# A graph network kernel on one core: the first two layers rearranged around edge counting

## What is computed

```python
h = relu(layernorm(x));  agg = segment_sum(h[src], dst)
x = x + relu((h + agg) @ L0_W1 + b1) @ L0_W2 + b2            # layer 0
h = relu(layernorm(x));  h = relu(h @ L1_W1 + b1) @ L1_W2 + b2   # hidden 64
x = x + h + segment_sum(h[dst], src)                          # layer 1
h = relu(layernorm(x))                                        # layer 2
cond = silu([sin(ph), cos(ph)] @ f_w1 + f_b1) @ f_w2 + f_b2   # ph: node_vec1 * 32 frequencies
for i in range(4):        # sparse attention over the edges, 4 heads
    y = norm(h) * (1 + cond @ s1_w + s1_b) + (cond @ b1_w + b1_b);  h = h + attention(y)
    y = the same with s2, b2;  h = h + relu(y @ m_w1 + m_b1) @ m_w2 + m_b2
x = x + h
x = x + L3(relu(layernorm(x)))   # 2 attention layers, 8 heads, edges turned round, then an MLP
```

## Time and profile before

| | us |
|---|---|
| median of 3 runs | 1182.97 (1182.5 to 1183.24) |
| profiled execution: its own time | 1185.03 |
| profiled execution: span | 1183.2 |
| mean granted clock of TensorE | 0.972 |
| busy: PE / weight loads | 1083.8 (92%) / 995.4 |
| busy: DVE / POOL / ACT | 809.2 (68%) / 710.6 (60%) / 548.9 (46%) |
| PE's share of the chain of waits that ended last | 65% |

### The profile page before, as it was taken

How to read it: one execution, slowest core, us unless ns; L and a number is a source line. 1 busy time by engine, 2 the same in 40 slices (tenths; PEclk the granted TensorE clock), 3 DMA queues, 4 the chain that set the end, 5 groups by cost and what they waited for, 6 DMA issues and landing times.

```text
span 1183.2 us, 20938 instructions
## 1 busy us (share of the span) xinstructions
PE 1083.8 (92%) x6814; PEld 995.4 (84%) x6814; DVE 809.2 (68%) x1562; ACT 548.9 (46%) x970; POOL 710.6 (60%) x960
## 2 busy tenths in 40 slices
...
GB/s 121 2 1 1 10 25 37 91 104 55 49 34 46 81 57 81 1 82 46 55 81 1 81 85 6 79 122 53 94 1 37 72 2 45 1 72 37 36 1 44
DMA packets 39358, 56.99 MB, mean 48 GB/s; under 512 B 13829, under 2 KB 14079, under 8 KB 38877
## 3 DMA queue, kind: packets, MB, share of 16 engines
...
## 4 chain that ended last, share of the span: by engine, by line
PE 65%; DVE 4%; POOL 4%; issue 2%; ACT 1%; POOLq 0%; DVEq 0%; ACTq 0%
PE ps L312 39%; PE ps L1610 8%; PE ps L334 7%; PE ps L1904 3%; PE ps L1923 3%; PE ps L2086 2%; PE ps L1870 1%; PE ps L1584 1%; POOL w_lo L352 1%; POOL prob L431 1%; ACT prob L408 1%; DVE prob L401 1%; POOL res L1291 0%; DVE acc L1809 0%; DVE acc L1807 0%
## 5 line engine op out<-in xcount | busy, mean ns | idle before, releaser
L352 POOL TENSOR_TENSOR w_lo<-w_raw,w_hi 128x512 fp32r<-128x512 f32 x152 | 202.8, 1334 | 12.7
L312 PE MATMUL ps<-yt_hi,w_hi 128*128 128x314 f32 x640 | 201.3, 314 | 4.0 <-DVE yt_lo L1988 3.8
L312 PE MATMUL ps<-yt_hi,w_lo 128*128 128x314 f32 x640 | 197.3, 308 | 0.0
L312 PE MATMUL ps<-yt_lo,w_hi 128*128 128x314 f32 x640 | 197.0, 308 | 0.0
L431 POOL TENSOR_SCALAR prob<-prob,rinv 125x628 f32<-125x628 f32 x160 | 126.9, 795 | 105.9 <-DVE rinv L416 87.0
L375 ACT ACTIVATE pt_hi<-ps 125x625 fp32r<-125x625 f32 x160 | 109.3, 694 | 103.2 <-PE ps L334 102.0
L349 POOL TENSOR_SCALAR w_hi<-w_raw 128x512 fp32r<-128x512 f32 x152 | 96.2, 633 | 71.1 <-DMA w_raw<-L_gnn_wo 38.4
L668 PE MATMUL ps<-oh_s,oh_d 125*125 125x314 bf16 x800 | 117.3, 303 | 23.5 <-DVE oh_s L564 17.7
L668 PEld LDWEIGHTS ps<-oh_s,oh_d 125*125 125x125 bf16 x800 | 105.8, 138 | 34.6 <-DVE oh_s L564 22.9
L312 PEld LDWEIGHTS ps<-yt_hi,w_hi 128*128 128x128 f32 x640 | 121.4, 190 | 6.5 <-issue 3.5
L312 PEld LDWEIGHTS ps<-yt_hi,w_lo 128*128 128x128 f32 x640 | 121.4, 190 | 0.0
...
## 6 DMA issues: line engine op xcount, KB each, us to landing
...
```

The source lines that it names most:

```text
L312: ins = pe.matmul(out_ap, lhs(i, kk), rhs(j, kk), start=kk == 0 and n == 0, stop=kk == count - 1 and n == 2)
L352: pool.tensor_tensor(w[slot][1][:, kk, 0:cols], w_raw[slot][:, kk, 0:cols], w[slot][0][:, kk, 0:cols].bitcast(FP32), ALU.subtract).then_in ...
```

## The change

**Counting takes side jobs** (table `SIDE`). In chunks 1 and 2 PE also transposes the tiles of h (job h), in chunks 2 to 5 it multiplies them with W1 (job u), ahead of the last eight groups of the chunk ("5" stands behind the last chunk). ACT and DVE split the results. The copies of h itself (L646 and the subtraction) go. Each chunk's first matmul waits for the side splits of the earlier chunks.

```diff
+    SIDE = ((1, "h", 0), (1, "h", 1), (1, "h", 2), (2, "h", 3), (2, "h", 4), (2, "u", 0), (3, "u", 1), (3, "u", 2),
+            (4, "u", 3), (5, "u", 4))
...
+    def act_side(act, c):
+        for i, kind, t in side_jobs(c):
+            source, high, _ = side_parts(i, kind, t)
+            act.wait_ge(s_xf, i + 1)
+            act.activation(high, source, ACT.Identity).then_inc(s_eh0, 1)
+    def dve_side(dve, c):
+        for i, kind, t in side_jobs(c):
+            source, high, lower = side_parts(i, kind, t)
+            dve.wait_ge(s_eh0, i + 1)
+            dve.tensor_tensor(lower, source, high.bitcast(FP32), ALU.subtract).then_inc(s_el0, 1)
+    def pe_side(pe, c):
+        for i, kind, t in side_jobs(c):
+            ap = side_bank(i)
+            if kind == "h":
+                pe.wait_ge(s_hn0, t + 1)
+                for b in range(C):
+                    ins = pe.transpose(ap[:, 128 * b:128 * b + R], res[:, t, b * 128:(b + 1) * 128], ident[0:R, 0:R])
...
+            if side_jobs(c):
+                pe.wait_ge(s_below, c * TILES)
+                pe_side(pe, c)
...
+        pe_side(pe, CHUNKS)
...
-    agg = pair("agg", "qk", [128, C, W])
-    MASKS_AFTER_G, MASKS_AFTER_F = ((0, 1), (2, 3), (4,), (5, 6)), ((7,), (8,), (9,), ())
...
-    tail = ["o0", "o1", "o2", "c1", "o3", "y0", "o4", "y1", "r", "y2", "y3", "y4", "ga", "c2"]
...
+    names1 = "b0 - b1 b2 - b3 - - b4 - g0 g1 c1 g2 g3 o0 o1 o2 c2 o3 y0 o4 y1 r y2 y3 y4 - ga".split()
+    names1 += "p0 p1 p2 p3 p4".split()
```

**Layer 0**: g is now u times the counts, so f, `agg` and `rtmp` go. ACT takes the relu in PSUM (`g_relu`). The embedding's inputs are loaded early; the embedding, c1, `act_one` and c2 move forward. Only five masks are made; the other five are transposes of them by PE (m0 to m4, `act_turned`), in the first norm. SP and POOL:

```diff
+    def first_sp(sp):
+        sp.wait_ge(s_xf, len(SIDE))
+        load_w(sp, 0, "L2_gnn_wv", 0, s_wl2)
+        sp.wait_ge(s_float, 2 * TILES)
+        sp.dma_start(noise[:, 0:N], a["node_vec1"].rearrange("n a -> a n").to_broadcast([64, N])).then_inc(s_noise, 16)
+        sp.dma_start(b2row[:], row(a["L0_gnn_b2"])).then_inc(s_row1, 16)
+        sp.dma_start(b1row[:], a["L1_gnn_b1"].rearrange("(a n) -> a n", a=1).to_broadcast([R, HID])).then_inc(s_row1, 16)
...
+    def first_pool(pool):
+        steps = Steps(s_p1)
+        pool.wait_ge(s_float, 2 * TILES)
+        pool.memset(noise[:, N:W], 0.0).then_inc(s_k, 1)
+        pool.memset(act1[:], 1.0).then_inc(s_k, 1)
+        pool.wait_ge(s_row1, 32)
+        for t in range(TILES):
+            pool.tensor_tensor(x[:, t, :], x[:, t, :], b2row[:], ALU.add).then_inc(s_xb1, 1)
+        for t in range(TILES):
+            steps.done(pool.tensor_scalar(ai(0, t), cnt[:, t, :], 1.0, 1.0, ALU.mult, ALU.mult))
             steps.wait(pool)
...
+        def rstd_of(t, count):
+            pool.wait_ge(s_st1, count + t + 1)
+            pool_rstd(pool, steps, t, s_rs1)
+        pool.wait_ge(s_wl2[0], 16)
+        for t in range(TILES):
+            rstd_of(t, 0)
+            if t in (1, 2):
+                split_weights(pool, steps, 0, s_wsp[0], [t - 1])
+        jobs1.wait_filled(pool, f"o{TILES - 1}")
+        pool.memset(r_nat[0][:, :, HID:ONES].bitcast(FP32), 1.0).then_inc(s_w2, 1)
+        pool.memset(r_nat[1][:, :, HID:ONES].bitcast(FP32), 0.0).then_inc(s_w2, 1)
+        pool.wait_ge(s_wsl, WS_DMAS * 16)
+        pool.wait_ge(s_wsz, 64)
+        split_ws(pool, steps)
+        split_weights(pool, steps, 0, s_wsp[0], [2])
+        jobs1.wait_filled(pool, "ga")
+        for part in yt:
+            pool.memset(part[:, :, N:W].bitcast(FP32), 0.0).then_inc(s_w2, 1)
```

The bias additions on x now stand ahead of the splits of the counts. ACT's order, cut:

```diff
+        def g_relu(c):
+            s = jobs1.wait_filled(act, f"g{c}")
+            act.activation(wide(s), wide(s), ACT.Relu, bias=b0c[:, c:c + 1]).then_inc(s_gr, 1)
+            act.wait_ge(s_gr, c + 1)
+            act.activation(halves(ft[0][:, c, :]), wide(s), ACT.Copy).then_inc(s_h1, 1)
...
+        act.wait_ge(s_ang, 1)
+        act.activation(emb[:], phase[:], ACT.Sin).then_inc(s_sin, 1)
+        g_relu(0)
+        g_relu(1)
+        s = jobs1.wait_filled(act, "c1")
+        act.wait_ge(s_fw, 14 * 16)
+        act.activation(halves(pre[:]), wide(s, 0, COND), ACT.Identity, bias=f_b1[:, 0:1]).then_inc(jobs1.drained[s], 1)
+        jobs1.wait_drained(act, "c1")
+        act.activation(sig[:], pre[:], ACT.Exp, scale=-1.0).then_inc(s_ex1, 1)
+        g_relu(2)
+        log(0)
+        g_relu(3)
+        log(1)
+        norm(0, 0)
+        norm(1, 0)
+        s = jobs1.wait_filled(act, "c2")
+        act.activation(halves(cond[:]), wide(s), ACT.Copy).then_inc(s_c2, 1)
+        log(2)
+        norm(2, 0)
+        y_hi(0)
+        norm(3, 0)
+        y_hi(1)
+        norm(4, 0)
+        y_hi(2)
+        log(3)
+        y_hi(3)
+        r_hi(0, 0, 3)
+        y_hi(4)
+        log(4)
+        r_hi(1, 3, 5)
+        act.wait_ge(s_m, TILES)
+        s = jobs1.at["ga"][0]
+        jobs1.wait_filled(act, "ga")
+        for half in range(2):
+            act.activation(gt[0][0:ONES, H2 * half:H2 * half + H2], ps[s][0:ONES, 512 * half:512 * half + H2],
+                           ACT.Identity).then_inc(s_h1, 1)
+    def act_first_norm(act, t):
```

DVE's order, cut:

```diff
+        for t in range(TILES):
+            b_lo(t)
+        embed_noise()
+        clamp(0)
+        g_lo(0)
+        g_lo(1)
+        act_one()
+        g_lo(2)
+        make_mask(0)
+        clamp(1)
+        g_lo(3)
+        make_mask(1)
+        dve.wait_ge(s_xb1, TILES)
+        residual("o0", 0)
+        residual("o1", 1)
+        residual("o1", 1)
...
+        residual("o2", 2)
+        make_mask(2)
+        y_lo(0)
+        residual("o3", 3)
+        clamp(3)
+        y_lo(1)
+        residual("o4", 4)
+        dve.wait_ge(s_row1, 32)
+        y_lo(2)
+        make_mask(3)
+        clamp(4)
+        y_lo(3)
+        r_part(0, 0, 3)
+        y_lo(4)
+        r_lo(0, 0, 3)
+        make_mask(4)
+        r_part(1, 3, 5)
+        jobs1_r = jobs1.at["r"][0]
+        dve.wait_ge(s_rsum, 2)
+        dve.sem_inc(jobs1.drained[jobs1_r], 1)
+        r_lo(1, 3, 5)
```

PE's, and the names of the first norm:

```diff
+            if c == 1:
+                pe.wait_ge(s_sin, 1)
+                pe.wait_ge(s_fw, 14 * 16)
+                condition("c1")
+        pe.wait_ge(s_ws0[1], C)
+        o_piece(0, (0,))
+        o_piece(1, (0,))
+        o_piece(0, (1,))
+        o_piece(1, (1,))
+        o_piece(2, (0, 1))
+        pe.wait_ge(s_a1, 1)
+        condition("c2")
+        o_piece(3, (0, 1))
-    first_norm = ["n1_0", "n1_1", "a1_0", "n1_2", "a1_1", "v0", "n1_3", "a1_2", "v1", "n1_4", "a1_3", "v2", "a1_4", "v3", "v4"]
+    first_norm = "- - n1_0 n1_1 m0 a1_0 m1 n1_2 m2 a1_1 v0 m3 n1_3 a1_2 m4 v1 n1_4 a1_3 v2 a1_4 v3 v4".split()
```

**Layer 1**: r comes in two parts (tiles 0 to 2, 3 and 4), each split on its own, and ga too. **First norm of layer 2**: ACT's normalisation adds up the mean on the way and a second pass the squares (R and Q), in place of DVE's statistics. POOL, DVE and ACT follow strings:

```diff
+        for op in "P0 P1 M0 P2 M1 S0 P3 M2 S1 P4 M3 S2 M4 S3 S4".split():
+            t = int(op[1])
+            if op[0] == "P":
+                pool_first_norm(pool, first, t)
+            elif op[0] == "M":
+                mean_of(t)
+            else:
+                first_rstd(t)
+        weights(first, 0, 0, 1, [3])
         weights(first, 1, 0, 1)
+        pool.wait_ge(s_sp, 16)
+        for part in pt:
+            pool.memset(part[:, :, N:W].bitcast(FP32), 0.0).then_inc(s_ptz, 1)
         weights(first, 2, 0, 1)
...
+        for op in "p0 p1 c0 p2 h0 c1 p3 h1 p4 l0 c2 h2 l1 b0 c3 h3 l2 b1 w0 c4 h4 l3 b2 w1 l4 b3 w2 b4 w3 w4".split():
...
+    def act_turned(act, t):
+        s = first_jobs.wait_filled(act, f"m{t}")
+        act.activation(mask3[:, t, 0:N].rearrange("p (a b) -> p a b", a=TILES), blocks(s, TILES, R), ACT.Copy,
+                       scale=SCALE3 / SCALE2).then_inc(first_jobs.drained[s], 1)
+        first_jobs.wait_drained(act, f"m{t}")
+        act.sem_inc(s_m3, 1)
...
+        for name in ("R0 Q0 R1 Q1 R2 m0 Q2 R3 a1_0 m1 Q3 R4 m2 a1_1 Q4 v0 m3 a1_2 m4 v1 a1_3 v2 a1_4 v3 v4").split():
```

1152 lines of the change are left out of this document (572 added, 580 removed).

## The result

The changed kernel takes **1207.2 us** (median of 4 runs, 1206.0 to 1208.9) against 1183.1 us before: a ratio of 1.0204 (95% interval 1.0186 to 1.0221), slower by 24 us. Timed again later beside a run of the kernel before at 1185.5, it took 1203.8 us, ratio 1.0153 (1.0114 to 1.0192). The forecast was 1190, in a range of 1177 to 1198. The direction was right, the size less than a third of what came (7 us against 24), and both medians lie above the range.

A forecast was written before the change was run, and what follows sets the result against it. Ahead of the first query matmul, chains of small steps over DVE, POOL and ACT were taken to bound time. Offsets 11.3 + 84.3 + 46.9 = 142.5 against 135.3 gave +7.2 us: profiled 1192, median 1190, range 1177 to 1198.

The forecast's parts named there:

- Counting: Edge counting on PE takes in the first weight product and h's transposes: its end moves by +11.3 us, to 152.1.
- L: The moment the last counting matmul ends, 140.8 us before the change; everything behind it is timed from there.
- the gap of 1.85: In edge counting, PE's wait of 1.85 us for a one-hot of ACT; claimed to go as ACT loses five copies.
- The interlocks: Layer's residuals, normalisations and y parts wait for each other on ACT and DVE: 5.2 us a tile, 39.2 together.
- The first norm: Norm ahead of the first attention block: 6.1 us a turn, 27.9 from first product p to first value matmul v0.
- The main case: The sum of the steps up to q0, the first query matmul: +7.2 us, 1190; chance 0.50, range 1185.5 to 1195.
- The embedding: Noise embedding on DVE between count tiles and g's splits: 10 us beside POOL's additions (3.9 alone, bounds 3.9 and 13).
- 1.5 MB land at + 42: Masks' spill, timed from the first p: leaves not before +34, lands at +42, wk's split to +50.3, no loss.
- behind it the two kernels issue the same work but for one table load: Behind the first query matmul (276.1 us before): same work, the extra table load of 1.28 us hidden.
- the one of looser interlocks: Rival: counting hides half its new work (-4), ga and r run at full clock (-4): 1182 to 1184; chance 0.15.
- The stall of counting: Rival: DVE waits for side splits and starts one-hots late, four chunk starts lose 1 us each: 1194; chance 0.15.
- POOL does not hold DVE: Faster rival: the embedding runs at 3.9 us instead of 10, about -10, 1180; chance 0.20.

The follow-up runs named there:

- a0: The changed kernel once more, unaltered, timed beside the follow-up experiments: 1203.8 us, ratio 1.0153 to the kernel before.
- e2: Changed kernel with POOL splitting wk ahead of its wait for the masks' spill: 1197.5 us, ratio 1.0088 to the kernel before.
- e12: Changed kernel with forty idle semaphore increments on PE in front of layer 0's output products, shifting its later instructions: 1201.9 us, ratio 1.0131 to the kernel before.
- e9: Changed kernel with the masks' spill cut into two transfers, rows 0 to 111 and 112 to 124: 1197.3 us, ratio 1.0100 to the kernel before.
- e13: Forty idle increments at the start of PE's stream, on the fastest kernel combining spill, weight-split and step-order edits: 1173.1 us, ratio 0.9897 to the kernel before.
- e7: Changed kernel with POOL starting its bias additions only when DVE's embedding is done: 1204.3 us, ratio 1.0156 to the kernel before.

## Where the prediction was right, and where it failed

**Right.** *Counting*: L moved by 10.2 us, forecast 11.3; the new split steps were covered and the gap of 1.85 was gone. *The interlocks*: third residual at L + 44.5 (forecast 45.1), 5.5 us a tile (5.2), 41.8 us from it to the first p (39.2). *The first norm*: 6.0 and 5.3 us a turn (6.1), 28.3 us from the first p to v0 (27.9), with the last piece of wv behind the norm, as said. The 2.6 us too many from the third residual to the first p are within the scatter: a0 has 39.2. The main case, slower by chains over DVE, ACT and POOL, is what happened up to v0.

**Off in size.** *The embedding* took 6.8 us, not 10: POOL's additions, which the forecast had begin with it, waited for their row until three steps were done. The first output matmul so came at L + 27.2 and not L + 32, at full clock. It was worth nothing, and that the third residual came on time is luck in part, two misses that cancel: DVE's steps from the end of the embedding to the first residual, most of them beside POOL, took 19.7 us where the forecast had 17.3, so that the first residual came at L + 36.2, against 36.8.

**Wrong, and the reason for the miss.** The step reads: "1.5 MB land at + 42 by the 5 to 6 us of a 1 MB load, and wk's split (4 x 2.0) follows, to + 50.3; the first k matmul wants it 3.5 behind q0 at + 46.9: no loss, but nothing left over." Three things in it failed. The transfer left at + 36.6, not + 34. On its 125 rows it took 13.6 us, not 8, since it ran on a third of the engines; the trace of before had the sign of it, and it was not read. This is the kernel before while it wrote the same masks:

```profile
222.00:225.00 3.00, 1.16 (x6) 1.02 (x5) 1.70 (x4) 0.00 (x0) 1.86 (x3) 0.50 0.30 126
```

A share of 0.30 and 126 GB/s: its 1.5 MB moved no faster there, but nobody waited for them. And the new wait was followed to POOL's next split alone, while PE's stream waits for the pads behind it ahead of q0. Together this is 2.6 us at q0, 3.8 at k0 and 1.9 for the clock that fell behind that wait, some 8 us in the trace. e2 took 6.3 us of them away by moving the split and e9 6.5 by the rows alone; no run did only these two together. The other failed step was "behind it the two kernels issue the same work but for one table load", with nothing put down for it: the same work took 3.4 us more. Of these 1.8 lie in the part with the two stops, which go when PE's instructions are shifted (e12, e13). The other 1.6 lie behind the sixtieth softmax step, stay in e13 (560.2 us against 558.4 before), and are open.

The profiled run lay 14 us above the forecast of 1192: 4.6 at q0, 5.7 from there to the first softmax step, 3.4 behind. The median lay 17 above: the forecast took off 2 us because the profiled run of before was slower than its median, and this one was 1.2 faster. Of the rivals, the one of looser interlocks got 1.1 of its 4 us at L and nothing else: r and ga ran at a granted clock of 0.50 to 0.58. The stall of counting did not come (each chunk's first matmul waited 0.3 us, for PE itself). That POOL does not hold DVE is refuted by e7.
